# A pre-norm attention and feed-forward block on one core: the two mixed slots with the first unit's output scaled, turned and projected by tile, and the third unit's loads in the first slot

## What is computed

```python
# decay per head: lam = exp(-slope_h); 16 heads of 32; chunks of 128 tokens
def step(S, inp):                      # one chunk, state S carried along the sequence
    qb, kb, vb = inp
    inter = einsum('bhcd,bhde->bhce', qb * decay_q, S)
    scores = einsum('bhcd,bhed->bhce', qb, kb) * dmask
    intra = einsum('bhce,bhed->bhcd', scores, vb)
    S_new = lam_c * S + einsum('bhcd,bhce->bhde', kb * decay_k, vb)
    return S_new, inter + intra

x = x + layernorm(attn(layernorm(x) @ w_qkv.T + b_qkv) @ w_out.T + b_out)
g = silu(quantised_matmul(layernorm(x), gate_w, gate_scale))
u = quantised_matmul(layernorm(x), up_w, up_scale)
x = x + layernorm(quantised_matmul(g * u, down_w, down_scale))   # weights rounded to float8 e4m3
```

## Time and profile before

| | |
|---|---|
| median of three runs | 993.68 us |
| the profiled execution | 993.01 us |
| its span, first to last instruction | 991.2 us |
| mean granted clock of PE | 0.995 |
| PE busy | 957.7 us, 97% |
| VectorE busy | 694.2 us, 70% |
| GpSimd busy | 686.9 us, 69% |
| ScalarE busy | 507.8 us, 51% |
| projections alone (`ahead`) | up to 243 us |
| the two mixed slots | 244 to 303 us |
| 16 slots with the feed-forward network | 303 to the end |

### The profile page before, as it was taken

How to read it: one execution, slowest core, us unless ns; L and a number is a source line. 1 busy time by engine, 2 the same in 40 slices (tenths; PEclk the granted TensorE clock), 3 DMA queues, 4 the chain that set the end, 5 groups by cost and what they waited for, 6 DMA issues and landing times.

```text
span 991.2 us, 21995 instructions
## 1 busy us (share of the span) xinstructions
PE 957.7 (97%) x8498; PEld 709.6 (72%) x8498; DVE 694.2 (70%) x1355; ACT 507.8 (51%) x985; POOL 686.9 (69%) x837
## 2 busy tenths in 40 slices
PE   7999999999887999999999999999999999999996
PEld 6777778776665776777677677767767776776764
DVE  6999998875878766767676676767667676765422
ACT  3656665565555544646354464635446463544522
POOL 2689999887666765859476585947658594765733
PEclk9999999999998999999999999999999999999999
DMA  9899899999598784837558383866838486612200
GB/s 314 214 274 271 257 276 294 283 255 289 150 203 202 151 163 92 192 72 175 120 131 165 87 192 79 167 124 132 182 66 191 85 166 125 128 55 43 39 28 22
DMA packets 297641, 159.88 MB, mean 161 GB/s; under 512 B 141632, under 2 KB 272832, under 8 KB 297408
## 3 DMA queue, kind: packets, MB, share of 16 engines
q1 hardware_dynamic: 296672, 157.86, 67.5%
q10 hardware_dynamic: 864, 0.61, 0.2%
HBM read 82.93 MB, written 41.94 MB: 126 GB/s over the span
## 4 chain that ended last, share of the span: by engine, by line
PE 58%; DVE 17%; issue 10%; POOL 9%; ACT 4%; DMA 1%; POOLq 0%; SPq 0%; DVEq 0%; ACTq 0%
PE bank L845 17%; PE bank L827 12%; PE bank L720 9%; PE bank L735 8%; PE att L720 7%; POOL att_pool L996 4%; DVE stats L1249 3%; DVE p L1290 3%; DVE state_hl L1320 3%; DVE w_pool L1380 2%; ACT w_pool L562 2%; POOL rstd L937 2%; POOL w_pool L1010 2%; PE att L804 2%; DVE state L1309 1%
## 5 line engine op out<-in xcount | busy, mean ns | idle before, releaser
L827 PE MATMUL bank<-f_pool,gate_q 128*128 128x256 f16 x1536 | 183.9, 273 | 4.5 <-ACT w_pool L562 4.1
L827 PE MATMUL bank<-f_pool,up_q 128*128 128x256 f16 x1536 | 183.5, 273 | 1.4
L845 PE MATMUL bank<-down_q,w_pool 128*128 128x512 f16 x768 | 168.3, 379 | 0.0
L827 PEld LDWEIGHTS bank<-f_pool,gate_q 128*128 128x128 f16 x1536 | 146.9, 98 | 26.8 <-ACT w_pool L562 6.7
L827 PEld LDWEIGHTS bank<-f_pool,up_q 128*128 128x128 f16 x1536 | 149.3, 98 | 22.1 <-DVE w_pool L1380 5.0
L996 POOL TENSOR_TENSOR att_pool<-p,att_pool 128x512 f16<-128x512 f32 x128 | 145.7, 1160 | 26.3 <-ACT att_pool L516 26.3
L1380 DVE SCALAR_TENSOR_TENSOR w_pool<-bank,us_t,w_pool 128x256 f32<-128x256 f32 x192 | 84.1, 480 | 112.5 <-PE bank L827 54.1
L934 POOL TENSOR_TENSOR rstd<-mv,eps_t 128x1 f32<-128x1 f32 (+1 forms) x112 | 30.0, 268 | 182.6 <-DVE mv L1252 182.6
L845 PEld LDWEIGHTS bank<-down_q,w_pool 128*128 128x128 f16 x768 | 74.0, 98 | 87.0
L1010 POOL TENSOR_TENSOR w_pool<-w_pool 128x512 f16<-128x512 f32 x96 | 111.3, 1163 | 28.8 <-ACT w_pool L568 28.8
L516 ACT CAST att_pool<-p 128x512 f16<-128x512 f32 x128 | 75.5, 615 | 56.4 <-DVE p L1290 56.4
(11 more groups left out here) (143 smaller groups left out, 1824.9 us busy)
## 6 DMA issues: line engine op xcount, KB each, us to landing
xr<-in_x SPq DMA_DIRECT2D x32, 512.0 KB, 4.6
dram_qk<-qk_hl SPq DMA_DIRECT2D x64, 256.0 KB, 3.4
att_pool<-dram_qk SPq DMA_DIRECT2D x64, 256.0 KB, 5.6
f_pool<-dram_qk SPq DMA_DIRECT2D x64, 256.0 KB, 5.6
dram_kd<-kd_hl SPq DMA_DIRECT2D x32, 256.0 KB, 3.0
dram_v<-vv SPq DMA_DIRECT2D x32, 256.0 KB, 3.5
qn_pool<-dram_qk SPq DMA_DIRECT2D x32, 256.0 KB, 6.3
out_x<-w_pool SPq DMA_DIRECT2D x32, 256.0 KB, 2.1
```

Of the source, the lines that this page charges most:

```text
L827: ins = nc.tensor.matmul(b[:, j * TOK:(j + 1) * TOK], w[:, k, o * P:(o + 1) * P], x1_hl[:, v % 2, part, k], start=(k == 0 and part == 0), ...
L845: ins = nc.tensor.matmul((b_gate, b_up)[t][:, :], h_hl[:, part, k, t * P:(t + 1) * P], down_q[:, k], start=(k == 0 and part == 0), stop=(k ...
```

## The change

`early` is replaced on every engine by two written-out lists, `first_slot` and `second_slot`. The operations are the same, and:

- `scale_o` takes a range of tiles, and unit 0 calls it once for each tile; `o_hi`, `o_lo`, `kd_hi`, `v_hi`, `kd_lo` and `probs_lo` get versions for one tile, half or block. `o_turned` becomes one semaphore for each tile; `project` and `x1_hi` wait for their own tile, for all units.
- Unit 0's turned output goes to `x1_hl[:, 1]` instead of `o_t`.
- PE, second slot: both `project_qk` 0 and 1 ahead of carry and state; `project(0)` tile 0, scores half, tile 1; `project_qk` 2 and 3 together ahead of `attend` 0.
- SP: the loads of unit 2 are spread over the first slot, between unit 14's spills and the two turns of unit 0's output; `load_xr(1)` comes after them.
- `scale_h` moves into `ahead(13)`. `kd_lo(15)` and `v_lo(15)` move on GpSimd from the second mixed slot into `slot(2)`, behind `h_lo(0, 0)`.

```diff
@@ sync
+            def turn_o_tile(s, t):
+                sp.wait_ge(o_lo_d, 2 * s + t + 1)
+                if s and t == 0:
+                    sp.wait_ge(out_mm, 2 * s)
+                    sp.wait_ge(v_mm, 2 * (LEAD + 1))
+                sp.dma_start_transpose(turned(o_mov(s).rearrange("p s k t -> p (s k) t"), t),
+                                       hl_1[:, t].rearrange("p s d -> p (s d)")).then_inc(o_turned[t], 16)
...
+            load_xr(0)
+            spill_v(LEAD - 1)
+            spill_q(LEAD)
+            sp.wait_ge(score_mm, 8)
+            load_unit(2, 0)
+            load_unit(2, 1)
+            turn_o_tile(0, 0)
+            spill_k(LEAD)
+            sp.wait_ge(state_mm, 2)
+            load_unit(2, 3)
+            turn_o_tile(0, 1)
+            spill_kd(LEAD)
+            spill_v(LEAD)
+            sp.wait_ge(carry_mm, 1)
+            sp.wait_ge(att_mm, 2)
+            load_unit(2, 2)
+            load_xr(1)
+            spill_q(LEAD + 1)
+            spill_k(LEAD + 1)
+            turn_x1(0)
+            turn_o(1)
@@ tensor
             def project(u, t):
+                pe.wait_ge(o_turned[t], 16 * (u + 1))
                 if t == 0:
-                    pe.wait_ge(o_turned, 32 * (u + 1))
...
+            def second_slot():
+                n = LEAD + 1
+                scores(1, 0, 0)
+                project_qk(n, 0)
+                project_qk(n, 1)
+                carry_and_state(1, 0)
+                project(0, 0)
+                scores(1, 0, 1)
+                project(0, 1)
+                project_qk(n, 2)
+                project_qk(n, 3)
+                attend(1, 0)
+                scores(1, 1, 0)
+                project_v(n, 0)
+                scores(1, 1, 1)
+                carry_and_state(1, 1)
+                project_v(n, 1)
+                attend(1, 1)
@@ scalar
+            def first_slot():
+                probs_hi(0, 0, 0)
+                v_hi(LEAD - 1)
+                q_hi(LEAD, 0)
+                probs_hi(0, 0, 1)
+                state_hi(0, 0)
+                q_hi(LEAD, 1)
+                k_hi(LEAD, 2)
+                probs_hi(0, 1, 0)
+                kd_hi_half(LEAD, 0)
+                k_hi(LEAD, 3)
+                probs_hi(0, 1, 1)
+                o_hi_tile(0, 0)
+                kd_hi_half(LEAD, 1)
+                v_hi_tile(LEAD, 0)
+                state_hi(0, 1)
+                v_hi_tile(LEAD, 1)
+
+            def second_slot():
+                q_hi(n, 0)
+                o_hi_tile(0, 1)
+                q_hi(n, 1)
+                probs_hi(1, 0, 0)
+                state_hi(1, 0)
+                y_normalise(0, 0)
+                probs_hi(1, 0, 1)
+                k_hi(n, 2)
+                y_normalise(0, 1)
+                k_hi(n, 3)
+                x1_hi(0, 0)
+                probs_hi(1, 1, 0)
+                x1_hi(0, 1)
...
@@ gpsimd
+            def first_slot():
+                state_decay(0, 0)
+                probs_lo(0, 0, 0)
+                probs_lo(0, 0, 1)
+                v_lo(LEAD - 1)
+                q_lo(LEAD, 0)
+                q_lo(LEAD, 1)
+                state_decay(0, 1)
+                probs_lo(0, 1, 0)
+                kd_lo_half(LEAD, 0)
+                probs_lo(0, 1, 1)
+                kd_lo_half(LEAD, 1)
+                v_lo(LEAD)
+
+            def second_slot():
+                state_decay(1, 0)
+                q_lo(n, 0)
+                probs_lo(1, 0, 0)
+                q_lo(n, 1)
+                inverse_std_of(LN_Y, 0, 0)
+                residual(0, 0)
+                probs_lo_block(1, 0, 2)
+                inverse_std_of(LN_Y, 0, 1)
+                probs_lo_block(1, 0, 3)
+                residual(0, 1)
+                inverse_std_of(LN_X1, 0, 0)
+                state_decay(1, 1)
+                inverse_std_of(LN_X1, 0, 1)
+                x1_lo(0, 0)
+                probs_lo(1, 1, 0)
+                x1_lo(0, 1)
+                probs_lo(1, 1, 1)
@@ slot(s)
                 h_lo(v, 0)
+                if v == 0:
+                    kd_lo(units - 1)
+                    v_lo(units - 1)
@@ vector
+            def first_slot():
+                masked(0, 0, 0)
+                carry_and_state(0, 0)
+                masked(0, 0, 1)
+                state_lo(0, 0)
+                k_lo(LEAD, 2)
+                masked(0, 1, 0)
+                out_sum(0, 0)
+                k_lo(LEAD, 3)
+                masked(0, 1, 1)
+                o_max(0, 0)
+                scale_o(0, slice(0, 1), 1)
+                v_sum(LEAD, 0)
+                o_lo_tile(0, 0)
+                carry_and_state(0, 1)
+                v_sum(LEAD, 1)
+                out_sum(0, 1)
+                o_max(0, 1)
+                scale_o(0, slice(1, T), T)
+                state_lo(0, 1)
+                o_lo_tile(0, 1)
+                masked(1, 0, 0)
+
+            def second_slot():
+                carry_and_state(1, 0)
+                y_moments(0, 0)
+                masked(1, 0, 1)
+                state_lo(1, 0)
+                y_moments(0, 1)
+                x1_moments(0, 0)
+                k_lo(n, 2)
+                x1_moments(0, 1)
+                k_lo(n, 3)
+                masked(1, 1, 0)
+                out_sum(1, 0)
+                masked(1, 1, 1)
+                v_sum(n, 0)
+                carry_and_state(1, 1)
+                v_sum(n, 1)
+                state_lo(1, 1)
...
```

More of the change, by code:

```diff
@@ L224, in x_mov, with o_mov @@
             return x_odd if n % 2 else o_t[:, :]
+        def o_mov(u):
+            return o_t[:, :] if u else x1_hl[:, 1]
         def x_landed(n):
@@ L672, in slot @@
                 y2_normalise(v, 0)
-            for s in range(units + 2):
-                if s < 2:
-                    early(s)
-                else:
-                    slot(s)
+            first_slot()
+            second_slot()
+            for s in range(2, units + 2):
+                slot(s)
             y2_normalise(units - 1, 1)
@@ L1412, in ahead @@
                     row_sums()
+                if k == LEAD - 1:
+                    scale_h()
                 k_lo(k, 2)
@@ L1494, in slot @@
                     o_max(s, 1)
[L1495 removed]
+                    scale_o(s, slice(0, T), s + 2)
                     state_lo(s, 1)
```

215 lines of the change are left out of this document (80 added, 135 removed).

## The result

| | before | after |
|---|---|---|
| median of five timed runs each, us | 993.26 (992.92 to 994.0) | 987.9 (987.59 to 988.59) |
| profiled execution / its span, us | 993.01 / 991.2 | 988.57 / 986.8 |
| busy us of PE, DVE, POOL | 957.7, 694.2, 686.9 | 958.7, 690.4, 687.6 |

The ratio is 0.994 (95% interval 0.9928 to 0.9953): 5.4 us faster, 4.4 in the profiled pair. PE is as busy as before, 1.0 us more even the earlier trace rows: what went are waits.

The account below looks back on a forecast made before the run. PE bounds the kernel, so only its waits can go: 16.0 us lost before, 8.8 plus 1.2 after, 6.0 gained; 993.01 becomes 987.0, and with 0.7 for the median 987.7 us. Own range 985.8 to 989.5, stated range 985.8 to 991.6.

Parts of the forecast that it names:

- first attention: First mixed slot, attention at 254.90: `scale_h` moved and low halves run first, so its 1.45 us wait goes.
- item 2: Second attention: PE ready at 264.4, the chain of mask, cast and low halves ends at 264.9; lost 0.5 us.
- item 3: Carry (1,0): waits for VectorE's `state_lo`, taken at the mean 1.8 us; lost 1.0 us, before 2.55.
- The page rule set beside item 3: Shared-port lock: `state_lo(0,1)` would begin only when `q_lo` ends, at 271.8, and the sum be 0.5 us smaller.
- The third unit's loads gain nothing in themselves: SP's loads of unit 2: they had landed in time, so moving them only clears SP and transfers in the third slot.
- Item 4: `project` of unit 0's turned output, behind SP's queue: tile 1 there at 276.4 to 278; lost 0.2 us, before 3.56.
- clock rival: Third slot: PE's idle time makes the clock fall again, costing 2.3 us, giving 990.0 us; chance 0.2.
- item 9: Third slot, second scores and second `gate_up`: VectorE's tail of unit 1 delays them; lost 2.9 us, before 1.2.
- GpSimd rival: Third slot: GpSimd becomes the bound, all its 4.6 us reach PE instead of 1.2, giving 991.1 us; chance 0.15.
- item 10: Third slot: moved `kd_lo(15)`, `v_lo(15)` delay GpSimd, so PE loses 0.6 us at `silu` and 0.6 at the next scores.
- the change does what it says: Denied by a rival: waits are only handed on, gain under 2.0 us, giving 992.7 us; chance 0.09.
- the fourth rival: `project`: turned tile 1 comes late, kernel slower past 284.9; 996 us if landing 10 us after issue; chance 0.04.

Follow-up runs that it names:

- filled kernel: Changed kernel with twenty unread matmuls filling PE's waits in the third slot, ten on each side of the second scores: 987.62 us, ratio 0.9932.

## Why the prediction was right, and where it was not

The forecast of 987.7 lies 0.2 from the 987.9, inside its own range, and the mechanism holds: PE's waits were the loss, and the change shortens nearly all of them by about as much as the replay said. Item by item, the time lost on PE as predicted and as the timeline has it (each from the start and the price of the block ahead):

| item | predicted | measured |
|---|---|---|
| 1 first attention (gain 1.45) | 0 | 0 (gain 1.46) |
| 2 second scores and attention | 0.5 | 1.84 |
| 3 carry (1,0) | 1.0 | 1.25 |
| 4 `project` | 0.2 | 0 |
| 5 attention (1,0) | 0.55 | 0.59 |
| 6 scores (1,1) | 0.9 | 0.76 |
| 7 last attention | 1.7 | 1.71 |
| 8 carry (2,0) | 0.95 | 0.98 |
| 9 second scores and `gate_up` | 2.9 | 2.92 |
| 10 `silu` later in the slot | 1.2 | 0 with the clock fallen; 1.18 in the filled kernel |

**The step that failed by size is in item 2.** It follows the mask, the casts and the low halves, and `state_lo(0,0)` has no price of its own in it. It took 4.28 us beside GpSimd's `v_lo` and `q_lo`, though the rows for it were at hand: item 3 names 4.35 beside a busy GpSimd and 1.15 beside an idle one, and item 2 did not ask the same of the other `state_lo` in the slot. The kernel with `state_hi(0,0)` first shows it: 1.16 us, no wait at the scores, 1.3 us off the median. In item 3 the same effect is a smaller miss, 2.12 for the 1.8 taken.

The page rule set beside item 3 (the Trainium skill, "SBUF — State Buffer", "SBUF: two separate sides": VectorE with two SBUF inputs and GpSimd hold the shared ports as a lock for a whole instruction) did better than the mean of the rows. Four `state_lo` operations took 4.28 us beside an unbroken row of passes of about 1.18, about one of them to each pass, and 1.18 beside none. Asked of every `state_lo`, it would have pointed at item 2.

**A sentence was wrong:** "The third unit's loads gain nothing in themselves". Put back, they cost 1.2 us, and not by landing late. They hold SP ahead of the turned `x1`. Item 4 counted SP's queue ahead of the o tiles; nobody counted it ahead of `turn_x1`, whose reader PE had come 7 us closer. The forecast did not suffer, since the change does move them.

**The clock rival came true in part.** The place was right (item 9's idle time, the second `gate_up`); the price was not. It said 2.3 us, and the profiled execution lost 1.67 at once and 0.5 at the end; the two groups of runs are 1.0 apart. It also does not come every time: the kernel with `state_hi(0,0)` first had the same waits and kept its clock. The GpSimd rival's 4.6 us did not reach PE: 1.2 did, in the filled kernel, as item 10 says. The turned tile 1, which the working had 0.2 us late, was in time by about 0.2: where PE waited for both tiles, `project` started 34.12 us after the first scores, and the changed kernel wants tile 1 at 34.35. The kernel that reaches `project` 1.24 us sooner already waits 1.03 for it. And the change does what it says.

The gain adds up so: 16.0 lost before, 10.05 in items 1 to 9 (8.7 predicted), a lead of 5.96 (7.2); then 1.67 of clock, which hid item 10's 1.2, a lead of 4.3; with 0.3 ahead of the first scores, which varies by more than that between kernels that are the same up to there, and 0.2 lost behind the slot 4.4, the profiled pair. Where the clock stays, 4.77 is left in the slot instead; the medians differ by 5.4. So the gain of 6.0 was put 0.6 too high, mainly by item 2, and before's median came out 0.4 lower this time (993.26 against 993.68): the agreement within 0.2 us is closer than the working deserves. Part of it is luck: against the profiled pair's 4.4 the 6.0 is 1.6 too high.

Slips in the working that change little: items 1 to 9 add to 8.7, and the sum takes 8.8. The losses listed for before add to 15.6 and not to 16.0; the missing 0.4 lies between 280.25 and 313.99, in the waits and the half clock there. And a tile that lands 10 us after its issue at 274.1 would be there at 284.1, short of the 284.9 from which the fourth rival counts the kernel slower.

## What to carry to other kernels

When PE is the bound and waits are handed from one engine to the next, replay each engine's whole list, and look up in the rows what each VectorE operation costs beside a busy GpSimd. Here `state_lo` and a scale on two numbers a partition waited for whole passes, a row maximum and the same scale on one number did not. Before moving work into an idle stretch of GpSimd, look at which such operations of VectorE fall into it: the places tried for the same two low halves lie up to 3 us apart. And when the consumer comes forward, count each DMA queue again ahead of every transfer that it reads, not only ahead of the one that was late.

## What the runs showed of the hardware

- Some small VectorE operations wait for whole GpSimd passes: 0.17 us became 1.08 for 128x2 elements, and `state_lo` took 1.16 to 1.18, 2.04 to 2.12 or 4.28 to 4.35 us with no pass, one to two, or an unbroken row of them beside it. Others don't: the same operations on 128x1 elements stayed at 0.15 to 0.21, the row maximum at 0.69, and VectorE's mask, which reads PSUM, at 0.6 to 0.7.
- The granted clock fell in the changed kernel behind waits of 1.22, 0.20 and 0.99 us close together, stayed at 1.00 behind the same three in the kernel with `state_hi(0,0)` first, and stayed there in the kernel before behind 3.56 idle us in one piece. Twelve of the fourteen traces show a stretch at half clock between 244 and 340 us; the two without are those of `state_hi(0,0)` first and of the filled kernel. Filling the stretch kept it up in one kernel and only moved the fall in another.
- A fall of the clock was worth less than the matmuls show where a wait for another engine followed: 1.67 us on the spot, 0.5 at the end of the slot (one pair of traces).
